# Plain scores over all 128 rows, with the two shift rows cleared by a small transfer per head

## The reference, cut to what matters

```python
qkv = x @ attn_qkvw + attn_qkvb              # heads of hd = 32
scores = jnp.einsum('bhqd,bhkd->bhqk', q, k) * scale
probs = jax.nn.softmax(scores, axis=-1)
ctx = jnp.einsum('bhqk,bhkd->bhqd', probs, v)
```

## Time and profile before

| what | us |
|---|---|
| median of 3 runs | 716.39 (715.22 to 716.9) |
| the profiled execution's own time | 716.33 |
| its span, first to last instruction | 714.5 |
| TensorE busy | 700.5 (98%) |
| VectorE busy | 470.8 (66%) |
| ScalarE busy | 424.0 (59%) |
| GpSimd busy | 288.7 (40%) |

### The profile page before, as it was taken

The page is one execution under the profiler, slowest core; times in us unless marked ns, Lnnn a source line. Parts: engine busy times, 40 slices in busy tenths (PEclk is TensorE's granted clock), DMA queues, the critical chain, the costliest instruction groups (busy, mean ns, idle before and its releaser), DMA issues.

```text
span 714.5 us, 11764 instructions
## 1 busy us (share of the span) xinstructions
PE 700.5 (98%) x3489; PEld 527.9 (74%) x3496; DVE 470.8 (66%) x833; ACT 424.0 (59%) x919; POOL 288.7 (40%) x209
## 2 busy tenths in 40 slices
PE   6999999999999999999999999999999999999996
PEld 5777678677676686786876866866767777888885
DVE  6887556575585574675656746557688679775573
ACT  4459567686685686766866867855467772221111
POOL 5793070171162153134125059836644834131120
PEclk9999999999999999999999999999999999999998
DMA  8666436336336345443643474845825332141101
GB/s 279 181 194 214 124 83 207 107 89 205 97 100 195 90 111 155 130 123 92 190 112 84 113 236 129 249 164 181 299 89 178 97 141 89 60 147 59 60 29 60
DMA packets 55732, 98.97 MB, mean 139 GB/s; under 512 B 10896, under 2 KB 21520, under 8 KB 54800
## 3 DMA queue, kind: packets, MB, share of 16 engines
q1 hardware_dynamic: 55408, 98.13, 44.8%
q10 hardware_dynamic: 288, 0.39, 0.2%
HBM read 56.41 MB, written 16.65 MB: 102 GB/s over the span
## 4 chain that ended last, share of the span: by engine, by line
PE 92%; issue 2%; DVE 2%; SPq 1%; DMA 1%; ACT 1%; POOL 0%; POOLq 0%; DVEq 0%
PE bank L471 58%; PE bank L599 8%; PE bank L568 8%; PE bank L613 8%; PE bank L720 4%; PE bank L746 2%; PE bank L524 1%; PE bank L735 1%; DMA w_raw<-in_wqkv 1%; SPq L228 1%; SPq L233 1%; PE bank L705 1%; ACT bank L883 0%; DVE columns L1422 0%; DVE c_raw L1394 0%
## 5 line engine op out<-in xcount | busy, mean ns | idle before, releaser
L1422 DVE TENSOR_REDUCE columns<-bank 128x1 f32<-128x512 f32 x256 | 172.3, 687 | 77.5 <-PE bank L568 77.4
L878 ACT ACTIVATE probs<-bank 128x512 f32<-128x512 f32 x256 | 152.6, 599 | 115.4 <-PE bank L599 112.8
L883 ACT ACTIVATE bank<-bank,columns 128x512 f32<-128x512 f32 x256 | 169.3, 661 | 21.0 <-DVE columns L1422 20.1
L471 PE MATMUL bank<-big_hi,w_hi 128*128 128x512 f32 x384 | 154.4, 402 | 6.2 <-DVE big_lo L1314 5.7
L471 PE MATMUL bank<-big_lo,w_hi 128*128 128x512 f32 x384 | 151.5, 395 | 0.0
L471 PE MATMUL bank<-big_hi,w_lo 128*128 128x512 f32 x384 | 150.7, 393 | 0.0
L568 PE MATMUL bank<-kp,qp 96*128 96x512 f32 x256 | 102.1, 399 | 0.8 <-ACT bank L883 0.8
L599 PE MATMUL bank<-qp,kp 128*128 128x512 f32 x256 | 100.7, 396 | 0.0
L471 PEld LDWEIGHTS bank<-big_hi,w_hi 128*128 128x128 f32 x384 | 73.3, 191 | 23.2 <-DVE big_lo L1314 7.0
L471 PEld LDWEIGHTS bank<-big_hi,w_lo 128*128 128x128 f32 x384 | 72.7, 189 | 16.9
L471 PEld LDWEIGHTS bank<-big_lo,w_hi 128*128 128x128 f32 x384 | 73.1, 190 | 15.5
(11 more groups left out here) (146 smaller groups left out, 1072.6 us busy)
## 6 DMA issues: line engine op xcount, KB each, us to landing
w_raw<-in_wqkv SPq DMA_DIRECT2D x7, 1536.0 KB, 8.6
c_raw<-in_ctx SPq DMA_DIRECT2D x16, 512.0 KB, 4.2
qp<-q_hi SPq DMA_DIRECT2D x128, 64.0 KB, 2.0
kp<-k_hi SPq DMA_DIRECT2D x124, 64.0 KB, 2.0
big_raw<-in_xT SPq DMA_DIRECT2D x16, 256.0 KB, 6.5
qp<-q_lo SPq DMA_DIRECT2D x64, 64.0 KB, 2.0
c_scratch<-c_q SPq DMA_DIRECT2D x16, 256.0 KB, 2.2
r_all<-r_scratch SPq DMA_DIRECT2D x64, 64.0 KB, 2.0
```

Source lines behind the costliest of these rows:

```text
L471: mm = nc.tensor.matmul(dst, lhs[a], rhs[b], start=(k == 0 and n == 0) if first is None else False, stop=(k == last_k and n == 2))
L878: nc.scalar.activation(probs[:, j, t, :], bank(ST0 + i % 2), ACT.Exp).then_inc(sem["exp_ok"], 1)
L883: nc.scalar.activation(bank(max_bank(s, n)), bank(max_bank(s, n)), ACT.Exp, bias=m_col[:, n:n + 1], accum_out=l_col[:, 1 - par, n:n + 1]). ...
L1422: nc.vector.reduce_max(m_col[:, n:n + 1], bank(max_bank(s, n)), AX, negate=True).then_inc(sem["rowmax"], 1)
```

## The change

The plain scores run over all 128 rows, from unit 1 on (in step 1, for unit 0, over 96 as before). The shift rows of `qp` must then be 0 while they are computed. For units 0 and 1 they are 0 from the memset; from unit 2 on each packing of a head's queries begins with a transfer that copies rows 98 and 99 of `qp` (zeros) over rows 96 and 97, for that head and that half. It counts on the same semaphore as the three packing transfers, so the numbers waited for grow. The wait for the memsets (`plus_ok`) moves in step 2 from the first transposed score to the first plain one.

```diff
-    PACK_INC = 6 * 16
+    PACK_INC, CLEAR_INC = 6 * 16, 16
...
+        def packs(units):
+
+            if isinstance(units, int) and units < 2:
+                return PACK_INC * units
+            return (PACK_INC + CLEAR_INC) * units - 2 * CLEAR_INC
...
                 if not isinstance(s, int) or s >= 2:
                     sp.wait_ge(sem["st_mm"], NS * (s - 2) + QT * (j + 1))
+                    if which == "q":
+                        sp.dma_start(qp[SHIFT:SHIFT + 2, par, j, :].bitcast(f32), qp[SHIFT + 2:SHIFT + 4, par, j, :].bitcast(f32)).then_inc(packed[j], CLEAR_INC)
                 for dst, row, src in parts:
...
                     if t == 0:
-                        pe.wait_ge(packed[j], PACK_INC * s)
+                        pe.wait_ge(packed[j], packs(s))
+                    if n == 0 and isinstance(s, int) and s == 2:
+                        pe.wait_ge(sem["plus_ok"], 3)
+                    rows = SHIFT if second else P
...
-                    nc.tensor.matmul(bank(max_bank(s, n)), qp[0:SHIFT, 1 - par, j, t * P:(t + 1) * P],
-                                     kp[0:SHIFT, 1 - par, j, :], start=True, stop=True).then_inc(sem["max_mm"], 1)
+                    nc.tensor.matmul(bank(max_bank(s, n)), qp[0:rows, 1 - par, j, t * P:(t + 1) * P],
+                                     kp[0:rows, 1 - par, j, :], start=True, stop=True).then_inc(sem["max_mm"], 1)
...
                         if isinstance(s, int) and s == 2:
-                            pe.wait_ge(sem["plus_ok"], 3)
                             pe.wait_ge(sem["vT_ok"], 2)
...
-                            wait_alone(dve, packed[h], PACK_INC * s)
+                            wait_alone(dve, packed[h], packs(s))
```

More of the change, by code:

```diff
@@ L400, in _ @@
             for j in range(HPG):
-                sp.wait_ge(packed[j], PACK_INC * UNITS)
+                sp.wait_ge(packed[j], packs(UNITS))
             load_tile(2)
```

## The result

The changed kernel takes 711.71 us (median of 6 runs, 710.60 to 713.36), the kernel before 716.16 on the same chip: a ratio of 0.9939, 95% interval 0.9929 to 0.9949. So it is 4.45 us faster, where 7.1 were forecast, and 0.1 us above the range. The profiled execution took 712.89 us (span 711.1), 3.4 less than that of before. An attention step that nothing disturbs came out as forecast. What is missing lies in waits that are new or have grown.

A forecast was written before the change was run, and what follows sets the result against it. TensorE's own pace was taken to bound the attention steps. 716.33 - 6.5 (rows) - 0.87 (stalls gone) + 0.2 (new waits) = 709.2 us, range 708.1 to 711.6.

The forecast's parts named there:

- Part 1: TensorE, plain scores of steps 2 to 16: 128 rows remove 0.027 us extra behind each of 240, 6.5 us gained.
- undisturbed step: Attention step without stalls, read in step 8: falls from 28.29 to 27.86 us.
- Part 2: SP queue, steps 2 to 15: four more transfers per step, 0.6 us each, cost nothing, covered by SP's idle time.
- the cover: SP slack in step 8: shift rows land over 2 us before their transposed score, some 1.9 left after the change.
- Part 3: Steps 7, 9, 11, 13: c_raw 0.84 us later puts GpSimd's w_lo behind VectorE's clip, ending stalls; -0.87 us.
- the first meeting: Step 7: GpSimd's first w_lo starts 0.25 us ahead of VectorE's clip, which takes 2.71 us; expected to go.
- this meeting: Sign of a wrong forecast: later c_raw makes VectorE's rounding (L1401) meet GpSimd's second w_lo; no size or chance.
- New waits: Chains not shortening with TensorE, notably steps 2, 3, 15, 16: 0.2 us lost, other end 1.6 us.
- Rows gain, but the meeting is moved: Rival: rows gain, but clip and w_lo still meet or meet elsewhere; 709.8, up to 711.5 us; chance 0.12.
- The others: Rivals: no row gain, 715.5 us (0.07); clears fill SP, 733 us (0.04); only some distances shorten, 712.5 us (0.04).

The follow-up runs named there:

- before_measures: Kernel before (96 rows, no clears) with late 2 MB load, rounding of steps 3 and 15 earlier, w_lo in halves; 715.09 us.
- combined: Changed kernel with one clear per unit, 2 MB load behind last shift rows, rounding of steps 3 and 15 earlier, w_lo in halves; 708.69 us.
- row_mix: Changed kernel without clears, plain scores over 128, 127, 96 and 64 rows for heads 0 to 3; one run, 735.79 us.
- c2_late: Changed kernel, all clears kept, with the 2 MB load of c2 issued behind the last shift rows instead of ahead; 712.16 us.
- one_clear: Changed kernel with a unit's four clears made one transfer, just ahead of the shift rows' store; 709.90 us.
- craw_early: Changed kernel, all clears kept, with the next step's c_raw loaded right behind the shift rows; 711.46 us.
- clears_only: Changed kernel with its clears and moved wait, but plain scores over 96 rows; 715.93 us, 1.0002 of the kernel before.
- after: The changed kernel itself, first measurement and profile; median 711.71 us, profiled execution 712.89 us.
- after_again: The changed kernel once more without an edit, for a second profile; 711.94 us.
- one_clear_halves: Changed kernel with one clear per unit and GpSimd's w_lo subtraction cut into two instructions; 710.27 us.

## Why the prediction was wrong

**Part 1 was right.** 0.027 us for each plain score: undisturbed step 27.87 us (27.86 forecast), and 6.4 us between before_measures and combined. row_mix says what it hangs on: a matmul over fewer than 128 rows among matmuls over all of them; why that costs time stays open. That 6.4 comes so near to 6.5 is in part luck: the two profiled executions differ by 0.8 us ahead of step 2, where both kernels compute the same. Read step by step the rows give 13 x 0.42 us in steps 3 to 15, 0.3 in step 16 and, by an estimate, 0.4 in step 2, together 6.2.

"TensorE: Matmul & The Clock Gate", section "LDWEIGHTS (loading the stationary operand)", of the Trainium skill says that a weight load takes as long over 32 rows as over 128. The page of before agrees for the loads themselves (188 ns over 96 rows, 189 over 128), but that there is nothing to gain, as would follow for the whole, the runs decide against here.

**Part 2 had the price right and the cover wrong.** The queue's instructions of L260:
```profile
L260 SPq DMA_DIRECT2D qp<-qp x56: 598/613/672, 59.3 to 444.4; - x56
```
0.61 us, as assumed. But the cover was read in step 8, an even step in which all went well, and "over 2 us" for the shift rows was carried to all steps. In step 6 the queue waited 2.4 us for one small store to land, and at the end the shift rows landed 4.9 us after their issue. Both times 1.5 or 2 MB had been issued ahead of them: with the 2 MB 9.1 us ahead (before) the rows landed in 2.9 us, with 7.1 us (changed kernel, both profiles) in 4.8 to 4.9. "DMA: Bandwidth & Descriptors", section "Two DMAs through the same engine are not ordered", of the Trainium skill says that within one queue of one DMA engine descriptors start in order; c2_late agrees, where the same two rows, issued ahead of the load, land in 1.8 to 2.0 us.

**Part 3 is the step that failed.** It took the fourth clear's delay of c_raw (0.84 us) as the end of the stalls: -0.87 us. For the first meeting it held: steps 9, 11, 13 and 15 lost nothing, with c_raw 1.0 us later. But it did not see that a still later c_raw brings the second w_lo onto the rounding. In step 7 c_raw came 2.9 us later (8.00 against 5.10), GpSimd's first work on it too, and the second w_lo 1.8 us later (19.74 us into the step, 17.94 before). The prediction named this meeting as what would prove it wrong and gave it neither price nor chance; steps 3, 5 and 7 lost 2.6 us in the profiled execution.

one_clear (fewer clears) and craw_early (same clears, early c_raw) remove it in steps 4 to 14 in two independent ways, and clears_only shows part 3's own gain beside it. The size follows the time of c_raw. In the odd steps 5 to 13 of after, after_again and c2_late, with c_raw 6.1 to 6.2 us into the step nothing is lost, with 6.6 to 6.7 it is 0.1 to 0.3 us, with 6.9 to 8.0 it is 0.5 to 1.6.

The trace of before had the meeting already. VectorE in its step 3, where c_raw goes out 6.67 us into the step:
```profile
97.46 1.22 DVE L1401 TENSOR_SCALAR c_q<-c_raw,consts 128x1024 bf16<-128x1024 f32 x1
```
That rounding falls behind a w_lo begun at 95.73, and the step took 28.40. The prediction read step 5 alone for what a later c_raw does. In step 3 of the changed kernel c_raw is no later than that (6.69): there the loss grew because the rounding comes 0.3 us sooner in a shorter step, onto the same w_lo (1.41 us).

"SBUF — State Buffer", section "SBUF: two separate sides", of the Trainium skill describes the lock, and the meetings agree: who starts second waits. Where VectorE waited, it was done 0.54 to 0.56 us after the GpSimd instruction that it met, so what counts is how much of that is left: 2.56, 2.71 and 2.93 us behind a w_lo just begun, 1.15 in step 5 of before behind a w_hi begun at 146.78, 0.82 in one_clear behind the end of another, 0.68 with nearly nothing left (craw_early). The other way round, GpSimd's w_lo takes 2.71 instead of 2.40 us where the clip was first (one_clear). So the later c_raw did not free the clip, it put it behind a GpSimd instruction of 1.05 us in place of one of 2.40.

**New waits** were set at 0.2 us with 1.6 as the other end. They were of another kind than those priced. The end of the kernel alone took 1.1. Step 2 kept its 25.9 us, since a plain score waits 0.86 us for ScalarE near its start (0.56 before). Where no such wait stands, in combined and one_clear_halves, step 2 takes 25.13 us, 0.76 less than before, of which 0.33 are that kernel's wait; so the rows do gain some 0.4 there. What sets these waits stays open: the other kernels over 128 rows took 25.5 to 26.4 us for it, the same code included (25.85 and 26.14 in the two profiles of the changed kernel).

**Rivals.** "Rows gain, but the meeting is moved" (709.8 to 711.5, 0.12) is what happened, at the upper edge and past it; its price was taken from a plain score's stall of 0.2 us, while a meeting at the end of a step costs up to 1.6, since there all products of the step are used up. The others fell.

**Why c_raw is late in one step and not in another** goes, in the loop, with when the store of reciprocals of the even step before lands. Steps 6, 8, 10 and 12 of after, after_again and c2_late are twelve cases. In seven the store landed 15.0 to 17.1 us into the step, and the next c_raw went out at 6.1 to 6.2; in three it landed at 17.5 to 17.7, and c_raw went out at 6.6 to 6.7; landed at 18.5 and 18.9, c_raw went out at 7.57 and 8.00. That loads issued ahead make the store slow is shown in part: craw_early takes the 0.5 MB of c_raw from ahead of it, and it lands in 1.6 to 1.9 us in odd steps (3.5 to 3.9 in the changed kernel) and in 6.0 to 6.5 in the even steps 4 to 12, which still have the 1.5 MB ahead (6.4 to 9.6 in the changed kernel). Not settled: why the landing varies so with the same loads ahead (no run moved the 1.5 MB), and why c_raw is late in step 5 (6.9 to 7.3 in those three) although that store landed by 17.1.

## What to carry to other kernels

In this kernel a matmul over fewer than all 128 rows between full ones cost 0.027 us of TensorE's time though its duration looked the same: read starts, and fill the rows with zeros if that can be had for one small transfer. Small transfers held the issuing queue by number, not bytes (0.61 us for 4 KB and for 16 KB), so clear everything at once, and put them where nothing timed hangs behind them. When an edit moves the work of an engine that shares a lock with another, list every pair that can now meet, not just the one that goes away, look in the trace of before for a step where they already do, and read the cover in the step where the largest load is on the queue.

## What was not expected of the hardware

- 127 rows cost what 96 do (0.027 us), 64 rows fifteen times as much (0.40 us). "TensorEngine Tiling (Array Packing)", section "Key Properties", of the Trainium skill says that a change of tiling mode drains TensorE, and 64 rows are one of the modes it lists; that this is what row_mix shows is argued, no run tells it apart.
- A clear of 16 KB (two rows of all four heads) holds SP 0.617 us, one of 4 KB 0.613.
- The store of the reciprocals issued at 171.03, 8 KB, could be read back at 180.75 only, the median landing of such a store being 4.4 us and the shortest 1.3; what is ahead of it on the queue differs.
